# Expert tiles fetched by whole rows through scratch memory instead of by quarters, and the last stage's first steps moved ahead

## The reference, cut to what matters

```
xn = layernorm(x)
s  = attention(xn)              # causal, 32 query heads, 8 key/value heads of 16, rotary embedding
g  = silu(experts(xn))          # 8 experts of 512x512, the best 2 of each token, relu, mean
x  = x + s * g
xn = layernorm(x)
s  = long_convolution(xn)       # taps from a state-space model, computed in the kernel
g  = silu(xn @ w_deq + bias)    # w_deq: weight times one scale a 128x128 block
out = x + s * g
```

## Time and profile before

| | |
|---|---|
| median of 3 runs | 689.17 us (687.06 to 692.37) |
| the profiled execution | 686.85 us, span 684.9 us |
| busy | PE 625.2, DVE 551.0, POOL 353.5, ACT 289.1 us |
| TensorE clock granted over the span | 0.979 of full |
| DMA | 92.67 MB, 135 GB/s on average |

### The profile page before, as it was taken

One profiled execution on the slowest core, in us unless ns is written; L12 is line 12 of the kernel. 1 busy time (PEld: TensorE's weight loads), 2 busy tenths in 40 slices (PEclk: granted clock), 3 DMA queues, 4 the chain that ended last, 5 costly groups with the idle time before them and its releaser, 6 DMA issues.

```text
span 684.9 us, 12390 instructions
## 1 busy us (share of the span) xinstructions
PE 625.2 (91%) x3574; PEld 338.8 (49%) x3574; DVE 551.0 (80%) x1790; ACT 289.1 (42%) x535; POOL 353.5 (52%) x497
## 2 busy tenths in 40 slices
PE   8899998698989999999999999998998999589997
PEld 5788784243433334333433343333443333378886
DVE  6688899668977788987888788787798873869995
ACT  4443226234344344443544444434453343345441
POOL 3777541537765723466464157664335614576630
PEclk9999999769999999999999999999999999899999
DMA  7599989355667455173562635627246327567841
GB/s 260 153 332 252 337 214 178 64 79 178 102 197 122 106 89 80 39 135 88 102 109 60 88 62 118 114 83 118 52 88 117 120 71 228 107 153 206 208 127 77
DMA packets 55567, 92.67 MB, mean 135 GB/s; under 512 B 10328, under 2 KB 23320, under 8 KB 55504
## 3 DMA queue, kind: packets, MB, share of 16 engines
q1 hardware_dynamic: 41890, 66.45, 41.5%
q0 software_dynamic: 8576, 18.62, 12.7%
q10 hardware_dynamic: 5038, 6.84, 4.0%
HBM read 61.93 MB, written 29.43 MB: 133 GB/s over the span
## 4 chain that ended last, share of the span: by engine, by line
PE 61%; DVE 24%; issue 6%; POOL 3%; DMA 2%; ACT 2%; another core or an unknown queue 1%; ACTq 1%; SPq 0%; DVEq 0%; POOLq 0%
PE bank L1685 15%; DVE bank L1406 12%; PE bank L1024 8%; PE bank L1657 7%; PE bank L1604 7%; PE bank L2150 6%; PE bank L1696 4%; PE bank L2155 4%; DVE arena L1406 2%; PE bank L1630 2%; PE bank L1641 2%; DVE m_parts L1419 2%; PE bank L1683 1%; PE bank L1001 1%; DMA arena<-xn_rows,slots_i 1%
## 5 line engine op out<-in xcount | busy, mean ns | idle before, releaser
L1406 DVE CUSTOM_DVE_ANT_0 bank<-bank,cst 128x384 f32<-128x384 f32 (+3 forms) x512 | 235.0, 522 | 52.4 <-PE bank L1604 44.2
L1527 ACT ACTIVATE arena<-bank 128x512 f32<-128x512 f32 x320 | 172.8, 601 | 193.8 <-PE bank L1630 121.4
L1356 POOL DMA_INDIRECT arena<-xn_rows,slots_i x156 | 150.4, 964 | 53.7 <-issue 40.1
L1343 POOL TENSOR_SCALAR_AFFINE_SELECT arena<-arena 128x512 f32<-128x512 f32 x128 | 80.8, 646 | 174.7 <-ACT arena L1527 174.0
L1685 PE MATMUL bank<-w_e,arena 128*128 x312 | 160.7, 621 | 0.0
L1604 PE MATMUL bank<-kt,qt 48*128 48x512 f32 (+1 forms) x496 | 113.8, 344 | 6.2 <-DVE arena L1406 6.1
L1604 PEld LDWEIGHTS bank<-kt,qt 48*128 48x128 f32 x496 | 71.8, 190 | 86.7 <-DVE arena L1406 46.2
L1657 PE MATMUL bank<-arena 128*32 128x512 f32 (+3 forms) x1024 | 87.3, 449 | 10.1 <-ACT arena L1527 8.3
L1630 PE MATMUL bank<-qt,kt 50*128 50x512 f32 x256 | 90.5, 458 | 1.1 <-DMA qt<-arena 0.7
L1685 PEld LDWEIGHTS bank<-w_e,arena 128*128 128x128 f32 x312 | 53.7, 191 | 57.2 <-issue 53.6
L1406 DVE DVE_READ_ACCUMULATOR2_ANT arena<- 128x1 f32 x512 | 73.0, 143 | 0.0
(11 more groups left out here) (172 smaller groups left out, 942.3 us busy)
## 6 DMA issues: line engine op xcount, KB each, us to landing
qt<-turned_parts SPq DMA_DIRECT2D x96, 128.0 KB
turned_parts<-qk_parts SPq DMA_DIRECT2D x8, 1280.0 KB
expert_rows<-arena SPq DMA_DIRECT2D x39, 256.0 KB
w_e<-in_L_ffn_W_e ACTq DMA_DIRECT2D x24, 256.0 KB, 6.4
kt<-turned_parts SPq DMA_DIRECT2D x96, 64.0 KB, 7.3
arena<-in_L_attn_x SPq DMA_DIRECT2D x16, 256.0 KB, 6.6
xn_rows<-arena SPq DMA_DIRECT2D x16, 256.0 KB, 6.6
w_e<-in_L_attn_x SPq DMA_DIRECT2D x16, 256.0 KB
```

The lines of the kernel that those rows point to most:

```text
L1343: g.affine_select(out=diag, in_=diag, compare_op=ALU.is_ge, fill=0.0, base=0, pattern=[[0, 2], [0, HALF], [1, P]], channel_multiplier=-1). ...
L1356: e.indirect_dma_start(xg[m % 2][:, n * P:(n + 1) * P], None, xn_q, bass.IndirectOffsetOnAxis(ap=slots_i[:, n, m:m + 1], axis=0)).then_inc ...
L1406: i = v.tensor_tensor_reduce(out=part, in0=part, in1=const("mask")[:, S - w:], scale=1.0, scalar=LOWEST, op0=ALU.add, op1=ALU.max, accum_o ...
L1527: nc.scalar.activation(pt[:, s, first:second + 1:second - first].rearrange("p c r q -> p c (r q)"), s2_bank(b, h, n).rearrange("p (c x) -> ...
```

## The change

POOL fetches the 128 rows of an expert tile with one indirect DMA of whole 2 KB rows into one of two spare tiles (`xr`, the last batch's third and fourth tile of `s_tok`). SP stores the tile to DRAM (`gathered_rows`), waits for that to land, and loads it back into `xg` with four DMAs, each of one quarter of the features (512 B pieces) into 32 partitions. `rows_plan` replaces `GATHERS`: for tile m it takes the place where tile m-2 is turned, puts the four loads at the next of two places in SP's stream (`shuffles`, before and behind `maximum_rows`), the store one place sooner, and the gather one place before that on POOL. The token numbers are used as they are, so `pe_tokens` and three DVE instructions of `dve_rows` go and one conversion stays. The last two pieces of `dft` move back by one group and one piece, since they overwrite `xr`.

At the seam to stage c: `rows` for tiles 0 and 1 move up to just behind the first select of the last group, `more_rows` of tile 0 behind the second; the copies to `c_slot` go; `rows` of tile 3 comes before `more_rows` of tile 2. On DVE `dve_scale` moves ahead of `dve_taps`; the high parts of the weight and `prepared` for tile 0 move ahead of the last group's `finish`; the low parts come behind the shift of tile 0.

```diff
+def rows_plan():
+    gathered, stored, loaded = {}, {}, {}
+    places = {m: (b * KV + h, slot) for (b, h, slot), tiles in TURNS.items() for m in tiles}
+    for m in range(MT):
+        g, slot = places[m - 2] if m > 1 else (0, 1)
+        q = 2 * g + 1 if slot == 0 else 2 * (g + 1)
+        loaded.setdefault(divmod(q, 2), []).append(m)
+        q -= 1
+        stored.setdefault(divmod(q, 2), []).append(m)
+        gathered.setdefault((q // 2, 0) if q > 1 and q % 2 else (max(q // 2 - 1, 0), 2), []).append(m)
...
-        def dve_rows(e, st):
+        def dve_rows(e):
             v = nc.vector
-            e.wait_ge(r_turned, 1)
-            quarters = compared[:, 0:KB * MT]
-            v.tensor_scalar(quarters, turned_tokens, float(KB), None, ALU.mult).then_inc(dve_steps, st.one())
-            e.wait_ge(dve_steps, st.count())
-            v.tensor_scalar(quarters, quarters, const("quarter"), None, ALU.add).then_inc(dve_steps, st.one())
-            e.wait_ge(dve_steps, st.count())
-            v.tensor_copy(slots_i.rearrange("p t m -> p (t m)"), quarters).then_inc(r_slot_rows, 1)
+            e.wait_ge(r_tokens, 1)
+            v.tensor_copy(slots_i[:, :], eid_f).then_inc(r_slot_rows, 1)
...
-            def gather(m, of_quarters=range(KB)):
+            def gather(m):
                 if m > 1:
-                    e.wait_ge(m_xt, m - 1)
+                    e.wait_ge(m_xs[m % 2], 16 * (m // 2))
...
-                for n in of_quarters:
-                    e.indirect_dma_start(xg[m % 2][:, n * P:(n + 1) * P], None, xn_q,
-                                         bass.IndirectOffsetOnAxis(ap=slots_i[:, n, m:m + 1], axis=0)).then_inc(m_x[m % 2], 16)
+                e.indirect_dma_start(xr[m % 2], None, xn_d, bass.IndirectOffsetOnAxis(ap=slots_i[:, m:m + 1], axis=0)).then_inc(m_x[m % 2], 16)
...
                     select(b, h, 0)
                     next_gather(b, h, 0)
+                    if (b, h) == (NB - 1, NG - 1):
+                        for u in range(2):
+                            rows(e, 0, u)
                     select(b, h, 2)
-                    next_gather(b, h, 1)
                     if (b, h) == (NB - 1, NG - 1):
-                        rows(e, 0, 0)
+                        more_rows(e, 0, 0)
...
                     if (b, h) == (NB - 1, NG - 1):
                         dve_tap_parts(e)
+                        dve_scale(e)
                         dve_taps(e, st)
+                        dve_scaled_high(e)
+                        prepared(e, st, 0)
                         finish(b, h)
-                        dve_scale(e)
...
         def sp_b(e):
+            def shuffles(b, h, place):
+                for m in LOADED.get((b * NG + h, place), ()):
+                    e.wait_ge(m_xs[m % 2], 16 * (m // 2 + 1))
+                    if m > 1:
+                        e.wait_ge(m_xt, m - 1)
+                    if m == 1:
+                        e.wait_ge(m_be, 9)
+                    rows = x_rows[m].rearrange("(n r) (c f) -> c r n f", n=KB, c=KB)
+                    for c in range(KB):
+                        e.dma_start(xg[m % 2][32 * c:32 * (c + 1), :].rearrange("r (n f) -> r n f", n=KB), rows[c]).then_inc(m_xl[m % 2], 16)
+                for m in STORED.get((b * NG + h, place), ()):
+                    e.wait_ge(m_x[m % 2], 16 * (m // 2 + 1))
+                    e.dma_start(x_rows[m], xr[m % 2]).then_inc(m_xs[m % 2], 16)
...
                     stores(b, h, 0, 1)
+                    shuffles(b, h, 0)
                     if b * NG + h + 1 < NB * NG:
                         maximum_rows(e, *next_group(b, h, 1), 0)
+                    shuffles(b, h, 1)
                     stores(b, h, 2)
...
-            TABLE = {1: (0,), 2: (1,), 3: (2, 3), 4: (4, 5), 5: (6, 7)}
+            TABLE = {1: (0,), 2: (1,), 3: (2, 3), 4: (4, 5), 5: (6,), 6: (7,)}
...
-            nc.gpsimd.tensor_copy(c_slot[:, u], slots[:, :, bass.ds(b * TPB + u, 1)]).then_inc(c_idx, 1)
-            e.wait_ge(c_idx, b * TPB + u + 1)
```

More of the change, by code:

```diff
@@ L99 @@
 TURNS = turns()
[L102 to L117, removed]
+def rows_plan():
[8 more added lines that the diff above has]
+        gathered.setdefault((q // 2, 0) if q > 1 and q % 2 else (max(q // 2 - 1, 0), 2), []).append(m)
+    return gathered, stored, loaded
+GATHERED, STORED, LOADED = rows_plan()
 COLS = {}
@@ L122 @@
 for _name, _n in (("ident", P), ("half", 1), ("eps", 1), ("minus", 1), ("mask", S), ("tri", P), ("cos", TPB * 8), ("sin", TPB * 8), ("s4", 16),
-                  ("lower", E * E), ("i128", NT), ("i128m", MT + 1), ("tile", MT), ("iota", P), ("tilenum", TOPK * NT), ("part", 1), ("sel", E), ("quarter", 1)):
+                  ("lower", E * E), ("i128", NT), ("i128m", MT + 1), ("tile", MT), ("iota", P), ("tilenum", TOPK * NT), ("part", 1), ("sel", E)):
     COLS[_name] = (_at, _at + _n)
@@ L615, in dve_a @@
             maxima(e, 0, 1, 2)
-            dve_rows(e, st)
+            dve_rows(e)
             maxima(e, 0, 1, 3)
@@ L1191, in pe_back @@
             i.then_inc(r_back, 1)
[L1193 to L1201, removed]
         qt = parts("qt", [P, 2, 2, HALF, S], "arena", 0)
@@ L1214, in build @@
         OT_END = used[0]
+        xr = [s_tok[:, NB - 1, u] for u in (2, 3)]
         xg = [take([P, D])]
@@ L1364, in go @@
                     next_gather(b, h, 0)
+                    if (b, h) == (NB - 1, NG - 1):
+                        for u in range(2):
+                            rows(e, 0, u)
                     select(b, h, 2)
-                    next_gather(b, h, 1)
                     if (b, h) == (NB - 1, NG - 1):
-                        rows(e, 0, 0)
+                        more_rows(e, 0, 0)
                     select(b, h, 3)
                     select(b, h, 1)
-                    if (b, h) == (0, 0):
-                        gather(0)
-                        gather(1)
                     next_gather(b, h, 2)
             def next_gather(b, h, slot):
-                for m, n in GATHERS[b, h, slot]:
-                    gather(m, (n,))
+                for m in GATHERED.get((b * NG + h, slot), ()):
+                    gather(m)
             values(0)
@@ L1801, in transform @@
                     c, k = divmod(n, KB)
+                    if n >= 6:
+                        e.wait_ge(m_xs[n % 2], 16 * ((MT + 1 - n % 2) // 2))
                     e.dma_start(dft[c][:, k, :], dft_d[c, k * P:(k + 1) * P]).then_inc(c_dft, 16)
@@ L1838, in build @@
         c_scale = take([P, KB, KB])
-        c_slot = take([P, TPB, TOPK, 1], U32)
         c_bias = be_f
@@ L1920, in inverse_root @@
                 g.tensor_tensor(c_rstd[:, u, :], c_mv[:, u, 1:2], const("half"), ALU.pow).then_inc(c_root[u % 2], 1)
-            rows(e, 0, 1)
-            for u in range(2):
-                more_rows(e, 0, u)
+            more_rows(e, 0, 1)
             rows(e, 0, 2)
             inverse_root(0, 0)
+            rows(e, 0, 3)
             more_rows(e, 0, 2)
-            rows(e, 0, 3)
             inverse_root(0, 1)
@@ L1942, in pool_c, with dve_inputs @@
                         inverse_root(b + (u + 3) // TPB, (u + 3) % TPB)
[L1944 to L1966 removed]
+        def dve_inputs(e, st):
             v = nc.vector
@@ L1994, in guarded, with prepared, dve_scale, dve_scaled_high @@
                 v.tensor_scalar(c_mv[:, u, 1:2], c_mv[:, u, 1:2], EPS, None, ALU.add).then_inc(c_stat[u % 2], 1)
+            return gated, layer_in, statistics, moments, guarded
+        def prepared(e, st, u):
+            gated, layer_in, statistics, moments, guarded = dve_inputs(e, st)
+            if u == 0:
+                e.wait_ge(b_s, TPB)
+            gated(0, u)
+            layer_in(0, u)
+            statistics(0, u)
+            moments(0, u)
+            guarded(0, u)
+        def dve_scale(e):
+            v = nc.vector
+            e.wait_ge(c_w, 48)
+            w4 = w_lin.rearrange("p k (o c) -> p k o c", o=KB)
+            sc4 = c_scale.rearrange("p o k -> p k o").unsqueeze(3)
+            for k in range(KB):
+                i = v.tensor_tensor(w4[:, k], w4[:, k], sc4[:, k].to_broadcast([P, KB, P]), ALU.mult)
+                i.then_inc(c_ws, 1)
+        def dve_scaled_high(e):
+            v = nc.vector
+            for par in range(2):
+                e.wait_ge(m_st[par], 16 * ((MT + 1 - par) // 2))
+            for k in range(KB):
+                e.wait_ge(c_ws, k + 1)
+                v.tensor_copy(w_high[:, k], w_lin[:, k]).then_inc(c_ws, 1)
+        def dve_scaled_low(e):
+            v = nc.vector
+            for k in range(KB):
+                e.wait_ge(c_ws, KB + k + 1)
+                v.tensor_tensor(w_low[:, k], w_lin[:, k], w_high[:, k].bitcast(F32), ALU.subtract).then_inc(c_ws, 1)
+        def dve_c(e, st):
+            v = nc.vector
+            gated, layer_in, statistics, moments, guarded = dve_inputs(e, st)
             def shift(b, u):
@@ L2052, in go @@
                         shift(*ahead)
-            def prepared(u):
```

(13 more changed lines are left out.)

41 lines of the change are left out of this document (10 added, 31 removed).

## The result

The changed kernel takes 700.15 us, the median of 4 runs (697.84 to 702.32), beside 688.12 for the kernel before (now 4 runs, 686.65 to 692.37): 1.0175 of before, 95% interval 1.014 to 1.0209. It is slower, and lies above the range that was forecast (678 to 697). Its profiled execution has a span of 698.9 us.

The account below looks back on a forecast made before the run. The prediction took TensorE (61% of the chain) and VectorE (24%) to bound the kernel, DMA only 2%. Terms -2.0 + 5.0 + 1.0 - 1.0 - 5.3 = -2.3 gave 686.9 us, range 678 to 697.

Parts of the forecast that it names:

- new DMAs on SP: Four loads and a store per tile, some ahead of the 12 query and key loads in odd groups: +5 us.
- slack of 0.9 us: At one odd group's first scores, DMA engines seemed done some 0.9 us before PE needed the 12 loads.
- 12.9 us: Delay from SP's added DMAs over the odd groups if the 12 loads had 0.9 us to spare.
- second rival: The 12 loads on SP's in-order queue pass their delay on to PE: 17.3 us, kernel 699.1 us; chance 0.14.
- The gathers: DVE's 2.7 us of waits for gathered rows at expert tiles should go; -2.0 us taken for PE.
- removed 113 us of POOL: 117 quarter gathers fewer on POOL, which has time to spare waiting for ACT: 0 gain by themselves.
- Selects and L1419: DVE's maxima instruction may meet POOL's selects more or less often without gathers: +1 us, bounds 0 to +5.
- rival in which every L1419 meets a select: POOL's selects hold DVE's maxima instruction each time: +5 us for +1, kernel 690.9 us; chance 0.11.
- hold by descriptor generation: By the skill page, the 117 removed gathers would also have held up DVE; some gain, not priced.
- Where the indices are made: 16 small matmuls and three DVE instructions become one, with PE's turn of keys behind: -1.0 us.
- The seam: At the passage to stage c, PE's 9.6 us of waits for normalised tiles shrink: -5.3 us.
- The round trip late: Tiles through gather, store and load land late for DVE in odd groups: 692 to 694 us; chance 0.06.

Follow-up runs that it names:

- e_tiny1: The kernel before, with one 512-byte DMA issued by SP ahead of the 12 stack loads in 11 odd groups; 680.6 us, ratio 1.0068.
- e_before: The kernel before, unchanged, run once more for its profile in a later set on chip 1; one run, 678.6 us.
- e_tiny: The kernel before, with four 512-byte DMAs issued by SP ahead of the 12 stack loads in 11 odd groups; 706.7 us, ratio 1.0464.
- e_tinyback: The kernel before, with four 512-byte DMAs issued by SP behind the 12 stack loads in 11 odd groups; 672.3 us, ratio 0.9957.
- e_behind: The changed kernel, with the second place's four loads and store behind the 12 stack loads in odd groups; 676.98 us, ratio 1.0001 of the kernel before.
- e_seam: The kernel before with only the change's last stage, expert rows still fetched by quarters; 669.7 us, ratio 0.991.
- after: The changed kernel itself, in its profile from the first comparison; 700.15 us, ratio 1.0175 of the kernel before.

## Why the prediction was wrong

- **The step that failed** is the term of the new DMAs on SP, taken at +5 between 0 and 22.8. It measured 24.5 us of waits and, by the clock, some 16 more. Three things were wrong in it. The slack of 0.9 us that I read out of the earlier trace rows holds for some groups only: in `e_tiny1`, with 0.6 us of delay, PE waited in 7 places (5.1 us), and in `e_before` it waited in 4 with none (2.1 us). Of the 12.9 us that were left with it I took 5, because the two groups of the earlier trace rows seemed the closest; ten groups waited. And the loads don't only take 4 x 0.474 us: they also wait for their store to land, behind `maximum_rows`, with the 12 loads behind them, 2.6 us more in one group and under 1 in the others. What the rows did show, both first scores at last issue + 7.4 us to within 0.01, was the right sign, and I priced it away. `e_tiny` and `e_tinyback`, the same DMAs ahead and behind, show that it is the place in the queue (1.0464 and 0.9957), and `e_behind` that it is this in the change (1.0001).
- **The clock was not in the sum at all.** Its cost is two fifths of the loss of the waits here (16 of 41 us). Seven of the ten waits, those of 2.05 to 4.43 us, had a stretch of 3 to 7 us at the lower level with them.
- **The second rival** had the mechanism and the sign right, SP's in-order queue ahead of the load that PE needs next, and a price of 17.3 us for waits of 24.5; I gave it 0.14. That its 699.1 us lies beside the measured 700.15 is luck: waits and clock came to some 41 us, and PE's other waits fell by more than it had (below).
- **The gathers.** DVE's waits for rows went, as said. PE's waits for exponentials fell by 8.3 us and not 2, and those for expert results, 5.0, which were in no term, went too; but `e_before` has only 4.8 of the first and none of the second, so how much of it is the change's is not shown. That the removed 113 us of POOL bring nothing by themselves held: POOL's idle time grew by as much.
- **Selects and L1419**: +1 was said. The waits for the turned maxima (L1641, 14.3 us) are 12.0 after, so it was nothing or a small gain, and the rival in which every L1419 meets a select did not come. The meetings moved one instruction on, to L1421, now L1401. By line (busy us, mean ns), before and after:

```profile
L1421 DVE SCALAR_TENSOR_TENSOR m_parts<-arena,m_parts 128x16 fp32r<-128x16 f32 x32 | 6.5, 204 | 1.1
```

```profile
L1401 DVE SCALAR_TENSOR_TENSOR m_parts<-arena,m_parts 128x16 fp32r<-128x16 f32 x32 | 11.6, 362 | 1.1
```

That is 5.1 us more; L1419 itself went from 15.0 to 11.2, 3.8 less. After, 16 of the 32 L1401 took over 0.25 us, and each of these ended 0.02 to 0.03 us behind a select; before, two took so long and one of them ended so. The Trainium skill's rule ("SBUF — State Buffer", "Who interferes with whom") stands by the row that it was held against. A hold by descriptor generation, which the prediction named beside it, hardly shows in the trace of before: beside a gather alone L1419 took 0.17 or 0.18 us in ten places and 0.35 or 0.36 in three, beside a select 0.25 to 1.22 in sixteen.

- **Where the indices are made**: -1.0 said. PE's wait for that piece of keys was 1.8 us and is 1.0: -0.8.
- **The seam**: -5.3 said. Waits of L2139 fell by 6.0 in the profile after, less 2.1 of a new one for a select; alone, `e_seam` gives 0.9% or 6 us. The size was right, and the first turned tile came without idle time, as forecast. The new wait was not forecast: `more_rows`, now among the selects, holds one of them up.
- **The round trip late** had 0.06. In the change itself POOL's 60.4 us behind stores cost PE no wait for a select (the one of 2.1 us is that of the seam); in `e_behind` they cost 6.5.

## What to carry to other kernels

Where an in-order queue issues the loads that an engine needs next, look whether the engine starts one landing time behind the last issue; if it does, a DMA put ahead of them, however small, costs most of its issue time (here 2.7 us ahead of the loads gave 1.9 of waiting a group), and its place in the queue matters more than its bytes. Price a wait of TensorE in a dense stretch at more than its length where rows show the clock falling with it (here 1.7 for 1). Before a load is queued behind a store's landing, see who stands behind both.

## What the runs showed of the hardware that I had not expected

- A DMA of 512 bytes between two DRAM tensors held SP for about 0.65 us (2.63 for four in `e_tiny`), one of 64 KB in 512-byte pieces for 0.44 (1.74 for four in the change).
- Four such small DMAs behind the 12 loads made the kernel before no slower, rather 0.4% faster (0.9931 to 0.9983). I have no cause for it.
- TensorE's grant stood at 0.50 for 3 to 7 us at each of 17 waits for these loads of 1.21 to 4.43 us (`after`, `e_tiny`, `e_tiny1`). At one of 2.37 us in `e_tiny` it did not move. At the nine waits of 0.27 to 0.96 us in `after`, `e_tiny1` and the one of 1.07 us in `e_before` it stayed at 1.00 for 5 us behind them.
